# Pass back of a two-direction scan: centring and output product as plain fp32 quarter products

## The chip, the cores and the metric

The kernel runs on one core of one Trainium2 chip. The metric is device time in microseconds of that core for the whole computation. The kernel before took 10529.74 us (median of 3 runs, 10524.03 to 10529.78).

## What is computed

Input is an image batch x of shape (4, 64, 256, 256) in fp32. Layer 0 is a group norm and a convolution block, added to x. Layer 1 is a group norm and two state-space blocks, along rows and along columns, fused by a 1x1 product and added to x. The part that the change touches is the second half of the state-space block, for each direction:

```python
def _s5_block(x, i, ...):
    fx = _layer_norm(x, ln1_g[i], ln1_b[i])
    h = _s5_scan(fx, ...)                      # forward and backward scan, C product, D * u
    x = jax.nn.gelu(h) + fx
    fx2 = _layer_norm(x, ln2_g[i], ln2_b[i])   # centring, variance, scaling
    return fx2 @ ff_enc[i].T @ ff_dec[i].T + fx2
...
y = jnp.concatenate([y_h, y_v], axis=1)
return jnp.einsum('bihw,oi->bohw', y, fusion_w) + fusion_b[None, :, None, None]
```

Everything behind the second layer norm is linear, so the kernel folds it into one 64x64 matrix W per direction, with the centring in it; it is applied to the value before the norm, and the result is multiplied by one over the deviation afterwards.

## The kernel before

The sequence of one image has 65536 pixels of 64 channels. A tile is 128 partitions by 512 columns: the channels of one pixel parity on partitions 0 to 63, those of the other on 64 to 127. A pixel's channel vector thus lies on one half of the partitions, and a matrix that acts on channels is block diagonal over 128 partitions.

For each of 4 images the program does layer 0 (`l0_*`), then for direction 1 (columns) and 0 (rows) a pass ahead (`pa_*`: first layer norm, input product, forward scan) and a pass back (`pb_*`). A pass back has M = 64 steps, four (`s`) to each of 16 groups (`n`); there are 8 pass backs, 512 steps. The order on every engine is written out by hand, and engines meet through semaphores with counted values.

A step m of the pass back on TensorE (`pb_pe`), in the order of issue: `first(m)` (L1726, 12 fp32r products of 128x128 weights `Dwr` over 512 columns), `var(m-2)` (L1301, four fp32 products of 32 weight columns each over 128 columns, one to each quarter of the output partitions), `bc(m-6)` (L1308, four products that spread one over the deviation), `second(m)` (L1739, 6 products with `Cwr`), and `center(m-1)`: two products with `ctrr` into ps2 (L1748) and three with `WWr` into ps6 or ps7 (L1753). An fp32 value goes through the array as fp32r in two parts, a high and a low one, and a product with split weights takes three (`PARTS`).

What goes into `center`: ScalarE (`pb_act`) does the gelu from the bank of L1739 into `x2` (L1814), VectorE (`pb_dve`, `add`) adds the normed input (L1874), ScalarE copies it rounded into `xp[0]` (L1831), VectorE (`low`) subtracts it to make `xp[1]` (L1880). What comes out: ScalarE squares the centred value into `sr` (L1820) for `var`, and moves W's output into one of eight slots of `tW` (L1827). When four steps' variances are there, ScalarE takes the root, VectorE makes `RS` (`deviations`, L1295 to L1297), `bc` spreads it, VectorE multiplies (`norm`, L1886), six steps (`LAG`) behind `add`. GpSimd (`pb_pool`) adds the result to `av` (`fin_v`, direction 1) or `ah` (`fin_h`, direction 0); `interleave` adds the bias and orders the pixels for the store. VectorE further does the backward scan (L1851), its rotation (L1670 to L1673) and the parts of `XP` for the next group.

The weights come from the set-up: `CC` holds them in fp32, `split` writes the two parts to `CP`, and SP stores these as `kc_d` and loads them for each pass (`pa_sp`). `ps` are the eight PSUM banks of 128 partitions by 512 fp32. Two lines of `center` carry what is changed:

```python
for x in range(2):
    ins = e.matmul(ps[2][:], ctrr[:], xp[x][:], start=(x == 0), stop=(x == 1))
...
for w, x in PARTS:
    ins = e.matmul(ps[6 + m % 2][:], WWr[:, w, :], xp[x][:], start=(w == 0 and x == 0), stop=(w == 1))
```

Of the kernel before, what the change touches and what calls it, by code (L numbers as in the profile page):

```python
# [18 lines left out]
M = 4 * NG  # L19
# [91 lines left out]
def build(nc, a, NB):  # L111
# [23 lines left out]
    ctrr = at("ctrr", [128, 128], F32R)  # L135
    En, Bc = at("En", [128, 129]), at("Bc", [128, 2048], F32R)
    lows = En[:, 128:129]
# [106 lines left out]
    WWr = at("WWr", [128, 2, 128], F32R)  # L244
# [20 lines left out]
    x2 = at("x2", [128, 512])  # L265
    xp = [at(f"xp{p}", [128, 512], F32R) for p in range(2)]
# [28 lines left out]
    LOADS = 26  # L295
    STORES = 11

    def setup_sp(e):
        for dst, src in [
                (sel[:], a["k_sel"]), (pm1[:], a["k_pm1"]), (C2[:], a["C2"]),  # L300
                (ctr, a["k_ctr"]), (En[:], a["k_E"]), (Bc0[:], a["k_Bc"]), (idn[:], a["k_id"]),
                (par[:], a["par"]), (Bt[:], a["Bt"]), (BB[:], a["BB"]), (Ct[:], a["Ct"]), (Dv[:], a["Dv"]),
                (wdw[:], a["wdw"]), (wd, a["wd42"]), (winT[:], a["winT"]), (fwT[:], a["fwT"]), (woT[:], a["woT"][128:HID, :]),
                (woT0[:], a["woT"][0:128, :]), (enc[:], a["enc"]), (decT[:], a["decT"]), (wfT[:], a["wfT"]),
                (fb[:], a["fb"]), (g2[:], a["g2"]), (b2[:], a["b2"]), (g1[:], a["g1"]), (b1[:], a["b1"])]:
            e.dma_start(dst, src).then_inc(sem["ld"], 16)
# [5 lines left out]
        for i, c in enumerate((slice(0, 2048), slice(2048, 4224))):  # L312
            e.wait_ge(sem["parts"], i + 1)
            for dr in range(2):
                for p in range(2):
                    e.dma_start(kc_d[dr, p, :, c], CP[p][:, dr, c].bitcast(F32)).then_inc(sem["kst"], 16)
        e.wait_ge(sem["LW"], 1)
# [4 lines left out]
    def setup_dve(e, own):  # L322
# [221 lines left out]
        split(2048, 4224, 2)  # L544
        step(e.tensor_copy(ctrr[:], ctr))
# [715 lines left out]
    def pa_sp(e, b, d):  # L1261
# [8 lines left out]
        for g in range(NG + 1):  # L1270
# [4 lines left out]
            if g == NG:  # L1275
                e.wait_ge(sem["ctr"], M * (f + 1))
                for p in range(2):
                    e.dma_start(Dwr[:, p, :].bitcast(F32), kc_d[d, p, :, 2048:4096]).then_inc(sem["kD"], 16)
                    e.dma_start(WWr[:, p, :].bitcast(F32), kc_d[d, p, :, 4096:4224]).then_inc(sem["kD"], 16)
# [19 lines left out]
    def variances(e, o, i, src):  # L1299
        for q in range(4):  # L1300
            ins = e.matmul(o[32 * q:32 * q + 32, 0:128], En[:, 32 * i:32 * i + 32], src[:, 128 * q:128 * q + 128],  # L1301
                           start=(i == 0), stop=(i == 3))
        return ins
# [18 lines left out]
    def pa_pe(e, b, d):  # L1322
# [14 lines left out]
        def var(g, i):  # L1337
# [5 lines left out]
            variances(e, ps[2], i, sq[:, i % 2, :]).then_inc(sem["var"], 1)  # L1343
# [242 lines left out]
    def pb_sp(e, b, d):  # L1586
# [9 lines left out]
        def load_v(n):  # L1596
            if n >= 2:
                e.wait_ge(sem[f"avs{n % 2}"], 16 * (8 * b + (n - 2) // 2 + 1))
            e.dma_start(av[n % 2][:].rearrange("p v h w -> p (v h w)"),
                        x1v_d[b, order[n]].rearrange("p c v h w -> (p c) (v h w)")).then_inc(sem[f"av{n % 2}"], 16)  # L1600

        def load_h(n):
            g = order[n]
            for p in range(2):
                if n >= 2:
                    e.wait_ge(sem["il"], M * b + 4 * (n - 2) + 2 * p + 2)
                for v in range(2):
                    e.dma_start(ah[n % 2][64 * v:64 * v + 64, p, :].rearrange("c (k r) -> c k r", k=16),
                                acc_d[b, :, p, :, v, 8 * g:8 * g + 8, :].rearrange("k c h w -> c k (h w)")
# [65 lines left out]
    def fin_v(e, b, m):  # L1675
        n, s = divmod(m, 4)
        e.wait_ge(sem["n2"], M * phase(b, 1) + m + 1)
        if s == 0:
            e.wait_ge(sem[f"av{n % 2}"], 16 * (8 * b + n // 2 + 1))
# [15 lines left out]
    def interleave(e, b, n, i):  # L1695
# [5 lines left out]
        x = ah[n % 2][64 * v:64 * v + 64, p, :].rearrange("c (k h w) -> c h k w", k=16, h=8)  # L1701
        y = oh[64 * p:64 * p + 64].rearrange("c h (k w v) -> c v h k w", k=16, v=2)[:, v]
        e.activation(y, x, ACT.Identity, bias=bias[64 * v:64 * v + 64]).then_inc(sem["il"], 1)

    def pb_pe(e, b, d):
# [5 lines left out]
        def first(m):  # L1711
            n, s = divmod(m, 4)
            if m == 0:
                e.wait_ge(sem["kD"], 64 * (f + 1))
# [40 lines left out]

        def var(m):
# [4 lines left out]
            variances(e, ps[4], s, sr).then_inc(sem["va"], 1)  # L1761
# [25 lines left out]
    def pb_act(e, b, d):  # L1787
# [9 lines left out]
        for m in range(M + 2 if d else M + 9):  # L1797
# [42 lines left out]
    def pb_dve(e, own, b, d):  # L1840
# [25 lines left out]
        def add(m):  # L1866
# [7 lines left out]
            e.scalar_tensor_tensor(x2[:], fi[n % 2][:, s, :], g1[:, d:d + 1], x2[:], ALU.mult, ALU.add).then_inc(sem["x2"], 1)  # L1874
# [19 lines left out]
        for m in range(M + 8):  # L1894
# [9 lines left out]
            if m < M:  # L1904
                low(m)
# [154 lines left out]
```

## Time and profile before

| | |
|---|---|
| median of 3 runs | 10529.74 us (10524.03 to 10529.78) |
| the profiled execution, its span | 10530.0 us |
| TensorE busy | 94% |
| VectorE busy | 82% |
| ScalarE busy | 54% |
| GpSimd busy | 17% |
| mean granted TensorE clock | 0.978 |

The profile is one execution, recorded by the hardware. PE is TensorE's products, PEld its weight loads, DVE is VectorE, ACT ScalarE, POOL GpSimd, SP SyncE. L and a number is a line of the kernel. A group line gives: line, engine, operation, written tile <- read tiles, the products' weights (rows * columns), shapes, xcount | busy us, mean ns of one | idle time of that engine just before them, and who ended it. A timeline line gives start us, duration us, engine, line, operation and count, and in brackets the idle time before it where there was some. Products overlap in the records, since each is shown from its start until it has left the array: the distance of two starts tells what a product costs, not its duration. A plain fp32 product appears as two records, an fp32r one as one.

### The profile page before, as it was taken

How to read it: one execution, taken by the hardware profiler on the slowest of the kernel's cores; microseconds unless marked ns; L12 is line 12 of the kernel's file. 1: busy time of each engine (PE TensorE's matmuls, PEld its weight loads, DVE VectorE, ACT ScalarE, POOL GpSimd, SP SyncE). 2: the span in 40 equal slices, each digit the busy share in tenths (PEclk: the TensorE clock that was granted, in tenths of full speed). 3: DMA queues.
4: the chain of work that ended last, by engine and by line, in shares of the span. 5: the costliest groups of instructions: out<-in, count | busy, mean ns of one | idle time of the engine just before them, and what ended most of it. 6: DMA issues, size and time to landing. Idle time of an engine off the chain costs nothing.

```text
span 10530.0 us, 160761 instructions
## 1 busy us (share of the span) xinstructions
PE 9857.4 (94%) x59942; PEld 7478.5 (71%) x59942; DVE 8606.3 (82%) x12871; ACT 5728.6 (54%) x9047; POOL 1787.3 (17%) x1824
## 2 busy tenths in 40 slices
PE   1999999999999999998989999899999999989998
PEld 1777766767777776675777777577677777757666
DVE  7788878978788887888878888888886888788787
ACT  0555544656655554454765555455575555446557
POOL 0000003333300001233320000223341000033333
PEclk9999999999999999999999999999999999999999
DMA  4667655465676765446567676534566666553555
GB/s 115 143 140 144 139 146 186 166 225 145 153 148 140 143 139 176 163 172 213 153 148 144 140 143 137 204 146 195 173 171 129 128 128 128 122 209 158 216 152 150
DMA packets 1276979, 1650.34 MB, mean 157 GB/s; under 512 B 837532, under 2 KB 1070380, under 8 KB 1174444
## 3 DMA queue, kind: packets, MB, share of 16 engines
q1 hardware_dynamic: 1276204, 1640.07, 58.6%
q8 instruction: 479, 7.85, 0.3%
q14 instruction: 296, 2.42, 0.1%
HBM read 786.71 MB, written 515.00 MB: 124 GB/s over the span
## 4 chain that ended last, share of the span: by engine, by line
PE 82%; DVE 11%; issue 2%; ACT 2%; DMA 1%; SPq 1%; POOL 1%; ACTq 0%; DVEq 0%; POOLq 0%
PE ps L819 14%; PE ps L1726 12%; PE ps L1739 7%; PE ps L789 6%; PE ps L1308 5%; PE ps L849 4%; PE ps L780 4%; PE ps L833 4%; PE ps L1753 3%; PE ps L1335 3%; DVE S L1508 3%; PE ps L1301 3%; PE ps L873 2%; PE ps L860 2%; PE ps L795 2%
## 5 line engine op out<-in xcount | busy, mean ns | idle before, releaser
L1131 DVE SCALAR_TENSOR_TENSOR F<-U,LW,F 106x512 f32<-106x512 f32 x2048 | 1536.0, 750 | 54.4
L1726 PE MATMUL ps<-fp,Dwr 128*128 128x512 f32 x6144 | 1471.4, 389 | 0.0
L1726 PEld LDWEIGHTS ps<-fp,Dwr 128*128 128x128 f32 x6144 | 1153.2, 188 | 239.6
L1109 DVE TENSOR_TENSOR Z<-ps,LW 128x340 f32<-128x340 f32 x1024 | 523.2, 511 | 822.7 <-PE ps L789 821.7
L943 ACT ACTIVATE XF<-ps 128x340 f32<-128x340 f32 x1024 | 464.5, 454 | 1116.2 <-PE ps L780 1116.2
L819 PE MATMUL ps<-P,WP 128*128 128x512 f32 x3072 | 905.7, 417 | 32.0 <-DMA H<-P 32.0
L819 PE MATMUL ps<-H,WP 128*128 128x512 f32 x3072 | 918.3, 421 | 0.0
L1308 PEld LDWEIGHTS ps<-RS,Bc 128*128 128x128 f32 x4096 | 573.8, 196 | 471.8 <-DVE RS L1297 228.4
L1739 PE MATMUL ps<-XP,Cwr 128*128 128x512 f32 x3072 | 829.8, 407 | 68.4 <-DVE XP L1863 68.4
L1308 PE MATMUL ps<-RS,Bc 128*128 128x128 f32 x4096 | 766.7, 312 | 132.0 <-DVE RS L1297 132.0
L1374 PE MATMUL ps<-fp,Bwr 128*128 128x512 f32 x3072 | 836.9, 410 | 20.4 <-DVE fp L1477 20.4
L1049 POOL TENSOR_SCALAR xo<-xo 64x512 f32<-64x512 f32 x4 | 6.0, 1499 | 4907.5 <-DVE xo L1165 4907.5
L1814 ACT ACTIVATE x<-ps,cst 128x512 f32<-128x512 f32 x512 | 351.4, 686 | 895.3 <-PE ps L1739 868.1
L1692 POOL TENSOR_TENSOR ah<-tW,ah 128x256 f32<-128x256 f32 x512 | 617.0, 1231 | 1057.9 <-DVE xp L1880 1035.8
L789 PE MATMUL ps<-XF,Rfwd 128*128 128x340 f32 x2048 | 754.4, 450 | 9.4 <-ACT XF L943 9.4
L995 ACT ACTIVATE xb<-P 64x1024 fp32r<-64x1024 f32 x512 | 541.6, 1058 | 332.4 <-DVE P L1099 325.0
L819 PEld LDWEIGHTS ps<-H,WP 128*128 128x128 f32 x3072 | 578.5, 188 | 175.5
L1682 POOL TENSOR_TENSOR av<-tW,av 128x512 f32<-128x512 f32 x256 | 493.3, 1932 | 1177.1 <-DVE xp L1880 1165.2
L1739 PEld LDWEIGHTS ps<-XP,Cwr 128*128 128x128 f32 x3072 | 553.4, 193 | 167.8 <-issue 77.8
L1874 DVE SCALAR_TENSOR_TENSOR x<-fx,g,x 128x512 f32<-128x512 f32 x512 | 382.8, 748 | 350.8 <-ACT x L1814 350.5
L780 PEld LDWEIGHTS ps<-WP,xb 128*128 128x128 f32 x4096 | 593.6, 191 | 96.9 <-issue 31.7
L971 ACT ACTIVATE U<-ps 106x390 f32<-106x390 f32 x768 | 381.5, 497 | 516.2 <-PE ps L833 505.6
(295 smaller groups left out, 21105.0 us busy)
## 6 DMA issues: line engine op xcount, KB each, us to landing
H<-P SPq DMA_DIRECT2D x512, 585.0 KB, 7.2
raw<-x SPq DMA_DIRECT2D x240, 640.0 KB, 11.6
fx_d<-fx SPq DMA_DIRECT2D x112, 1024.0 KB, 3.9
fl_d<-fp SPq DMA_DIRECT2D x112, 1024.0 KB, 5.3
fp<-fl_d SPq DMA_DIRECT2D x112, 1024.0 KB, 6.2
fx<-fx_d SPq DMA_DIRECT2D x112, 1024.0 KB, 5.4
x1h_d<-xo SPq DMA_DIRECT2D x256, 256.0 KB, 9.0
x1v_d<-xo SPq DMA_DIRECT2D x512, 128.0 KB, 7.9
```

Of the source, the lines that this page charges most:

```text
L780: ins = e.matmul(ps[6][:, HID * j:HID * j + HID], xb[t % 2][:, k:k + 128], w(p, W_FR, HID), start=(p == 0), stop=(p == 1))
L789: e.matmul(ps[6][:, 0:2 * HID], Rfwd[:], XF[n % 2][:], start=True, stop=True).then_inc(sem["fs"], 1)
L819: e.matmul(ps[2 + i][:], w(pw_, W_CONV + 128 * j, 128), m, start=(j == 0 and pw_ == 0 and px == 0), stop=False)
L995: ins = e.activation(dst, src, ACT.Copy)
L1109: e.tensor_tensor(Z[t % 2][:, 2 * c:2 * c + 2, :].rearrange("p a b -> p (a b)"), ps[6][:, 0:2 * HID], Wt, ALU.mult).then_inc(sem["z"], 1)
L1131: ins = e.scalar_tensor_tensor(o, u, wd[0:106, i:i + 1], o, ALU.mult, ALU.add)
L1308: ins = e.matmul(o[:, 128 * q:128 * q + 128], Bc[:, c:c + 128], RS[:, m % 2, :], start=True, stop=True)
L1374: ins = e.matmul(o[:], Bwr[:, w, 128 * (2 * s + j):128 * (2 * s + j) + 128], fp[g % 2][x][:, s, :], start=(s == 0 and w == 0 and x == 0), ...
L1682: e.tensor_tensor(o, t, o, ALU.add).then_inc(sem["finv"], 1)
L1692: ins = e.tensor_tensor(o, t, o, ALU.add)
L1726: ins = e.matmul(bank(m)[:], Dwr[:, w, c:c + 128], fq[n % 2][x][:, s2, :], start=(s2 == 0 and w == 0 and x == 0), stop=False)
L1739: ins = e.matmul(bank(m)[:], Cwr[:, w, c:c + 128], XP[x][:, j, :], start=False, stop=(j == 1 and w == 1))
```

## The change

Centring and W become plain fp32 products of 64x64, one for each half of the partitions. Centring takes rows 0 to 63 to output partitions 0 to 63 and rows 64 to 127 to 64 to 127; W takes rows 0 to 63 to output partitions 64 to 127 and the other way round, so the four products lie in four different quarters of the array. The value is kept in fp32 in two buffers `X2`, the high and low parts `xp` go, and with them L1831 and L1880. Since W swaps the two pixels of a tile, `variances` gets its own selection matrix `Es` in the pass back, and the loads of `av` and `ah` and the `interleave` swap the halves too. W's weights are stored and loaded whole instead of in parts.

```diff
-    ctrr = at("ctrr", [128, 128], F32R)
+    ctq = at("ctq", [128, 128])
+    Es = at("Es", [128, 128])
-    WWr = at("WWr", [128, 2, 128], F32R)
+    Wq = at("Wq", [128, 128])
-    x2 = at("x2", [128, 512])
-    xp = [at(f"xp{p}", [128, 512], F32R) for p in range(2)]
+    X2 = [at(f"x2{i}", [128, 512]) for i in range(2)]
-    LOADS = 26
-    STORES = 11
+    LOADS = 28
+    STORES = 13
@@ setup_sp
+        for dr in range(2):
+            e.dma_start(kc_d[dr, 0, :, 4096:4224], CC[:, dr, 4096:4224]).then_inc(sem["kst"], 16)
@@ setup_dve
-        split(2048, 4224, 2)
-        step(e.tensor_copy(ctrr[:], ctr))
+        split(2048, 4096, 2)
+        step(e.tensor_copy(ctq[:], ctr))
@@ pa_sp
-                    e.dma_start(WWr[:, p, :].bitcast(F32), kc_d[d, p, :, 4096:4224]).then_inc(sem["kD"], 16)
+                e.dma_start(Wq[:], kc_d[d, 0, :, 4096:4224]).then_inc(sem["kD"], 16)
@@ pb_sp, load_v
-            e.dma_start(av[n % 2][:].rearrange("p v h w -> p (v h w)"),
-                        x1v_d[b, order[n]].rearrange("p c v h w -> (p c) (v h w)")).then_inc(sem[f"av{n % 2}"], 16)
+            for p, hf in ((0, slice(64, 128)), (1, slice(0, 64))):
+                e.dma_start(av[n % 2][hf].rearrange("c v h w -> c (v h w)"),
+                            x1v_d[b, order[n], p].rearrange("c v h w -> c (v h w)")).then_inc(sem[f"av{n % 2}"], 16)
@@ pb_pe, center
-            e.wait_ge(sem["xp"], M * f + m + 1)
+            e.wait_ge(sem["x2"], M * f + m + 1)
             if m:
                 e.wait_ge(sem["sr"], M * f + m)
-            for x in range(2):
-                ins = e.matmul(ps[2][:], ctrr[:], xp[x][:], start=(x == 0), stop=(x == 1))
-            ins.then_inc(sem["cc"], 1)
             if m >= 2:
                 e.wait_ge(sem["tw"], M * f + m - 1)
-            for w, x in PARTS:
-                ins = e.matmul(ps[6 + m % 2][:], WWr[:, w, :], xp[x][:], start=(w == 0 and x == 0), stop=(w == 1))
+            for hf in (slice(0, 64), slice(64, 128)):
+                ins = e.matmul(ps[2][hf, :], ctq[hf, hf], X2[m % 2][hf, :], start=True, stop=True)
+            ins.then_inc(sem["cc"], 1)
+            for hf, other in ((slice(0, 64), slice(64, 128)), (slice(64, 128), slice(0, 64))):
+                ins = e.matmul(ps[6 + m % 2][other, :], Wq[hf, hf], X2[m % 2][hf, :], start=True, stop=True)
             ins.then_inc(sem["w"], 1)
@@ pb_act
-                if m:
-                    e.wait_ge(sem["xp"], M * f + m)
-                e.activation(x2[:], ps[{2: 3, 3: 5}.get(m, m % 2)][:], ACT.Gelu_apprx_tanh, bias=cD[:, 4 * d + s:4 * d + s + 1]
+                if m >= 2:
+                    e.wait_ge(sem["w"], M * f + m - 1)
+                e.activation(X2[m % 2][:], ps[{2: 3, 3: 5}.get(m, m % 2)][:], ACT.Gelu_apprx_tanh, bias=cD[:, 4 * d + s:4 * d + s + 1]
-            if m < M:
-                e.wait_ge(sem["x2"], M * f + m + 1)
-                e.activation(xp[0][:], x2[:], ACT.Copy).then_inc(sem["xp0"], 1)
@@ pb_dve
-        def low(m):
-            e.wait_ge(sem["xp0"], M * f + m + 1)
-            if m:
-                e.wait_ge(sem["w"], M * f + m)
-            e.tensor_tensor(xp[1][:], x2[:], xp[0][:].bitcast(F32), ALU.subtract).then_inc(sem["xp"], 1)
@@ pb_pool
-            e.wait_ge(sem["xp"], M * phase(b, d) + min(m + LAG + 1, M))
```

## Rows read from the trace of the kernel before

**Rows 1.** The page: busy time by engine, and the clock in 40 slices.
```profile
PE 9857.4 (94%) x59942; PEld 7478.5 (71%) x59942; DVE 8606.3 (82%) x12871; ACT 5728.6 (54%) x9047; POOL 1787.3 (17%) x1824
...
PEclk9999999999999999999999999999999999999999
```

**Rows 2.** Busy time in two pass-back stretches (stretch, length, busy us per engine, clock, DMA).
```profile
1779.00:2166.00 387.00, 383.53 (x2150) 296.81 (x2151) 335.32 (x471) 228.87 (x368) 111.41 (x58) 1.00 0.39 153
2433.00:2820.00 387.00, 383.07 (x2152) 296.19 (x2152) 323.35 (x471) 294.54 (x423) 146.05 (x129) 1.00 0.55 150
```

**Rows 3.** Timeline of TensorE over two steps of a pass back.
```profile
1806.03 1.58 PE L1739 MATMUL ps<-XP,Cwr 128*128 128x512 f32 x6
1807.45 0.61 PE L1748 MATMUL ps<-xp,ctrr 128*128 128x512 f32 x2
1807.90 0.84 PE L1753 MATMUL ps<-xp,WWr 128*128 128x512 f32 x3
1808.59 2.88 PE L1726 MATMUL ps<-fp,Dwr 128*128 128x512 f32 x12
1811.40 0.43 PE L1301 MATMUL ps<-sr,En 128*32 128x128 f32 x8
1811.75 0.66 PE L1308 MATMUL ps<-RS,Bc 128*128 128x128 f32 x4
1812.25 1.58 PE L1739 MATMUL ps<-XP,Cwr 128*128 128x512 f32 x6
1813.67 0.61 PE L1748 MATMUL ps<-xp,ctrr 128*128 128x512 f32 x2
...
1819.89 0.61 PE L1748 MATMUL ps<-xp,ctrr 128*128 128x512 f32 x2
```

**Rows 4.** Timeline around L873 and, narrow windows, in L873 and L1301.
```profile
1006.44 0.57 PE L780 MATMUL ps<-WP,xb 128*128 128x170 f32 x4
1006.74 0.28 PE L780 MATMUL ps<-WP,xb 128*128 128x170 f32 x1
1006.95 1.08 PE L873 MATMUL ps<-F,LW 128*64 128x512 f32 x4
1006.95 0.65 PE L873 MATMUL ps<-F,LW 128*64 128x512 f32 x2
1007.43 0.60 PE L873 MATMUL ps<-F,LW 128*64 128x512 f32 x2
1007.96 0.96 PE L876 MATMUL ps<-FQ,WO 106*128 106x512 f32 x3
1008.75 0.73 PE L789 MATMUL ps<-XF,Rfwd 128*128 128x340 f32 x2
...
2004.22 0.32 PE L1301 MATMUL ps<-sr,En 128*32 128x128 f32 x4
2004.35 0.29 PE L1301 MATMUL ps<-sr,En 128*32 128x128 f32 x4
```

**Rows 5.** Groups of products by line, and two lines' durations min/median/max.
```profile
L1748 PE MATMUL ps<-xp,ctrr 128*128 128x512 f32 x1024 | 319.1, 393 | 31.2 <-DVE xp L1880 31.2
L1335 PE MATMUL ps<-xin,Mb 128*128 128x512 f32 x1024 | 552.5, 643 | 12.2 <-DMA xin<-x1v_d 12.1 <-ACT xc L1422 0.2
...
L1748 PE MATMUL ps<-xp,ctrr x1024: 387/389/627, 1779.5 to 10493.6; 128*128 128x512 f32 x171
L1335 PE MATMUL ps<-xin,Mb x1024: 590/592/1222, 1517.7 to 10054.5; 128*128 128x512 f32 x171
```

**Rows 6.** Timeline where TensorE waits in a pass back, and the scans.
```profile
1779.48 0.74 PE L1748 MATMUL ps<-xp,ctrr 128*128 128x512 f32 x2 [0.64 <-DVE xp L1880]
1784.92 0.96 PE L1748 MATMUL ps<-xp,ctrr 128*128 128x512 f32 x2 [1.89 <-DVE xp L1880]
1997.37 3.92 DVE L1851 TENSOR_TENSOR_SCAN S<-RR,S 64x512 f32<-64x512 f32 x2
2165.33 0.73 PE L1748 MATMUL ps<-xp,ctrr 128*128 128x512 f32 x2 [0.80 <-DVE xp L1880]
2170.85 3.80 PE L1308 MATMUL ps<-RS,Bc 128*128 128x128 f32 x16 [2.98 <-DVE RS L1297]
2433.35 0.73 PE L1748 MATMUL ps<-xp,ctrr 128*128 128x512 f32 x2 [1.51 <-DVE xp L1880]
2438.79 0.73 PE L1748 MATMUL ps<-xp,ctrr 128*128 128x512 f32 x2 [1.92 <-DVE xp L1880]
2442.78 0.74 PE L1748 MATMUL ps<-xp,ctrr 128*128 128x512 f32 x2 [0.45 <-DVE xp L1880]
```

**Rows 7.** Groups of the copy and the subtraction.
```profile
L1831 ACT ACTIVATE xp<-x 128x512 fp32r<-128x512 f32 x512 | 325.2, 635 | 285.9 <-DVE x L1874 285.5
L1880 DVE TENSOR_TENSOR xp<-x,xp 128x512 fp32r<-128x512 f32 x512 | 353.0, 689 | 96.4 <-ACT xp L1831 76.2
```

More of the change, by code:

```diff
@@ L300, in setup_sp @@
                 (sel[:], a["k_sel"]), (pm1[:], a["k_pm1"]), (C2[:], a["C2"]),
-                (ctr, a["k_ctr"]), (En[:], a["k_E"]), (Bc0[:], a["k_Bc"]), (idn[:], a["k_id"]),
+                (ctr, a["k_ctr"]), (En[:], a["k_E"]), (Es[0:64], a["k_E"][64:128, 0:128]), (Es[64:128], a["k_E"][0:64, 0:128]), (Bc0[:], a["k_Bc"]), (idn[:], a["k_id"]),
                 (par[:], a["par"]), (Bt[:], a["Bt"]), (BB[:], a["BB"]), (Ct[:], a["Ct"]), (Dv[:], a["Dv"]),
@@ L311, in setup_sp @@
             e.dma_start(tb_d[dr], TB[:, dr].rearrange("p a b -> p (a b)")).then_inc(sem["kst"], 16)
-        for i, c in enumerate((slice(0, 2048), slice(2048, 4224))):
+        for i, c in enumerate((slice(0, 2048), slice(2048, 4096))):
             e.wait_ge(sem["parts"], i + 1)
@@ L1297, in deviations, with variances @@
         e.scalar_tensor_tensor(RS[:, m % 2, :], rh[:].bitcast(F32), lows, rs[:], ALU.mult, ALU.add).then_inc(sem[out], 1)
-    def variances(e, o, i, src):
+    def variances(e, o, i, src, pick):
         for q in range(4):
-            ins = e.matmul(o[32 * q:32 * q + 32, 0:128], En[:, 32 * i:32 * i + 32], src[:, 128 * q:128 * q + 128],
+            ins = e.matmul(o[32 * q:32 * q + 32, 0:128], pick[:, 32 * i:32 * i + 32], src[:, 128 * q:128 * q + 128],
                            start=(i == 0), stop=(i == 3))
@@ L1342, in var @@
                 e.wait_ge(sem["sd"], NG * f + g)
-            variances(e, ps[2], i, sq[:, i % 2, :]).then_inc(sem["var"], 1)
+            variances(e, ps[2], i, sq[:, i % 2, :], En).then_inc(sem["var"], 1)
         def bc(g, i):
@@ L1606, in load_h @@
                     e.wait_ge(sem["il"], M * b + 4 * (n - 2) + 2 * p + 2)
-                for v in range(2):
-                    e.dma_start(ah[n % 2][64 * v:64 * v + 64, p, :].rearrange("c (k r) -> c k r", k=16),
-                                acc_d[b, :, p, :, v, 8 * g:8 * g + 8, :].rearrange("k c h w -> c k (h w)")
+                for v, hf in ((0, slice(64, 128)), (1, slice(0, 64))):
+                    e.dma_start(ah[n % 2][hf, p, :].rearrange("c (k r) -> c k r", k=16),
+                                acc_d[b, :, 1 - p, :, v, 8 * g:8 * g + 8, :].rearrange("k c h w -> c k (h w)")
                                 ).then_inc(sem[f"ah{n % 2}"], 16)
@@ L1678, in fin_v @@
         if s == 0:
-            e.wait_ge(sem[f"av{n % 2}"], 16 * (8 * b + n // 2 + 1))
+            e.wait_ge(sem[f"av{n % 2}"], 32 * (8 * b + n // 2 + 1))
         o = av[n % 2][:].rearrange("p v (j s) w -> p s v w j", s=4)[:, s]
@@ L1700, in interleave @@
                 e.wait_ge(sem["ost"], 32 * (NG * b + n))
-        x = ah[n % 2][64 * v:64 * v + 64, p, :].rearrange("c (k h w) -> c h k w", k=16, h=8)
+        hf = slice(64, 128) if v == 0 else slice(0, 64)
+        x = ah[n % 2][hf, p, :].rearrange("c (k h w) -> c h k w", k=16, h=8)
         y = oh[64 * p:64 * p + 64].rearrange("c h (k w v) -> c v h k w", k=16, v=2)[:, v]
-        e.activation(y, x, ACT.Identity, bias=bias[64 * v:64 * v + 64]).then_inc(sem["il"], 1)
+        e.activation(y, x, ACT.Identity, bias=bias[hf]).then_inc(sem["il"], 1)
     def pb_pe(e, b, d):
@@ L1713, in first @@
             if m == 0:
-                e.wait_ge(sem["kD"], 64 * (f + 1))
+                e.wait_ge(sem["kD"], 48 * (f + 1))
                 e.wait_ge(sem["sq"], M * (f + 1))
@@ L1760, in var @@
                 e.wait_ge(sem["se"], NG * f + n)
-            variances(e, ps[4], s, sr).then_inc(sem["va"], 1)
+            variances(e, ps[4], s, sr, Es).then_inc(sem["va"], 1)
         def bc(m):
@@ L1873, in add @@
                     e.wait_ge(sem["nn"], M * (f + 1))
-            e.scalar_tensor_tensor(x2[:], fi[n % 2][:, s, :], g1[:, d:d + 1], x2[:], ALU.mult, ALU.add).then_inc(sem["x2"], 1)
-        def low(m):
-            e.wait_ge(sem["xp0"], M * f + m + 1)
-            if m:
-                e.wait_ge(sem["w"], M * f + m)
-            e.tensor_tensor(xp[1][:], x2[:], xp[0][:].bitcast(F32), ALU.subtract).then_inc(sem["xp"], 1)
+            e.scalar_tensor_tensor(X2[m % 2][:], fi[n % 2][:, s, :], g1[:, d:d + 1], X2[m % 2][:], ALU.mult, ALU.add
+                                   ).then_inc(sem["x2"], 1)
         def norm(m):
@@ L1903, in pb_dve @@
                 norm(m - LAG)
-            if m < M:
-                low(m)
             if s == 0 and n + 1 < NG:
```

2 rows, old and new, of the table SEMAPHORES are left out of this document.

## The prediction

> **What bounds the kernel now.** I read the page first: busy shares, then the clock line [rows 1]. TensorE is busy 94% of the span, VectorE 82%, ScalarE 54%, and the clock stands at its upper level (2.4 GHz) nearly throughout. Shares do not say what one stage waits for, so I took two pass-back stretches by themselves [rows 2]: in 387.0 us TensorE is busy 383 us, VectorE 335 and 323, ScalarE 229 and 295. Each stretch is one of eight pass backs (4 images, 2 directions) of 64 steps; all the change's work lies in these 512 steps. The timeline of TensorE in two neighbouring steps [rows 3] shows a fixed pattern with no wait printed: 12 products of L1726, the variances L1301, the spreading L1308, 6 products of L1739, then centring L1748 and W L1753. From 1807.45 to 1813.67 is 6.22 us, and so is the next. In steady state the step is the sum of TensorE's own work: what is added there is paid in full, what is taken from ScalarE or VectorE is not earned. Waits of TensorE stand only at the ends of a pass back [rows 6].
>
> **What TensorE gives up.** Per step 2 + 3 fp32r products of 128x128 weights over 512 columns. By the timeline they hold TensorE from 1807.45 to 1808.59 = 1.14 us, 0.227 each [rows 3]. Nothing lies beside them.
>
> **What it gets instead.** Four plain fp32 products with 64 rows and 64 columns: two on the diagonal quarters (centring, bank ps2), two on the other quarters (W, bank ps6 or ps7). No row of before has a product on a quarter; this is the disputed term, so it is bounded.
> - Alone: fp32 records come in two per product, and L1335 costs 552.5 us for 512 products, 1.08 us each [rows 5]. Four one after another, each at 1.08: 4.3 us.
> - Side by side: L873 is two fp32 products of 64 columns over 512, in the two column halves. In the narrow looks [rows 4] two records of different halves are under way together from 1006.95, and the other two from 1007.43. So the column halves work at the same time, in two waves 0.48 us apart. L1301 does the same with four tiles of 32 columns: four records at 2004.22, four at 2004.35 [rows 4]. The four quarters are also four tiles; if they behave like these four, they too need two waves.
> - The price of such a visit is more than its waves. Around L873 [rows 4]: the four L780 start at 1006.44 to 1006.74, 0.10 apart, but L873 starts 0.21 after the last, so 0.11 is lost going in; L873 holds the engine 1.01 (1006.95 to 1007.96); then three L876 take 0.79 to the next start against 3 x 0.227 = 0.68, so 0.11 is lost coming out. Sum 1.23 us. L1301 behind L1726 agrees in kind: 12 products from 1808.59 should be over at 1811.31, and it starts at 1811.40 [rows 3].
>
> I take the two waves and 1.22 us (each of the three differences is good to 0.01), since L873 and L1301 are the nearest rows (same type, same 512 columns, tiles below full width). A quarter has half the rows of L873, so a slightly shorter drain is possible, and two more weight loads per wave, so a slightly longer entry; I let these cancel. Step: 1.22 - 1.14 = +0.08 us. Over 512 steps: **+41 us**. The bounds around it: the waves alone, without entry and exit, are 2 x 0.43 = 0.86 (the 0.43: an fp32 record lasts 592 ns against 389 for an fp32r one [rows 5], 0.203 longer than one that is spaced 0.227), which is 0.28 less than now; with the full 0.37 of L873 and 0.15 more for four weight loads it is 1.38, 0.24 more.
>
> Beside this, "TensorEngine Tiling (Array Packing)" of the Trainium skill, Key Properties, says that changing the tiling mode drains TensorE, and that tiles then work independently. The trace agrees: the 0.11 us on either side of L873 are such changes, and they speak against this change, which adds two per step. Without them the term would be a gain.
>
> **What leaves the other engines.** ScalarE loses the copy L1831 (512 x 635 ns), VectorE the subtraction L1880 (512 x 689 ns) [rows 7]. In steady steps both lie beside TensorE's work: worth 0. The value is double-buffered, so gelu L1814 waits for W of two steps earlier instead of the subtraction; worth 0 too. With them the path gelu, add, centring is 0.64 + 0.69 = 1.32 us shorter, which counts where TensorE really waits for it. That is 31.2 us in all, before L1748 [rows 5]: at the start of a pass back 0.64 + 1.89, or 1.51 + 1.92 + 0.45, and 0.80 at its end [rows 6]. At the start the two small steps fall away before the pair of scans of 3.9 us [rows 6] that VectorE does between the first two values, so the second value gains twice and these waits should go: 31.2 - 8 x 0.80 = 24.8 us. At the end the wait of 0.80 goes, but centring itself tells ScalarE later (two fp32r took 0.61 to their end, two waves take 1.08 as in L873 [rows 4]), 0.47 later; the chain to the last deviations (L1308 waits 2.98 us for RS [rows 6]) keeps only some 0.3, 8 times, 2.6 us. Together **-27 us**. Late next at the start: TensorE itself.
>
> **What is moved or small.** Centring now also waits for tw of two steps earlier ahead of itself; behind it on TensorE stand W and the next L1726, but tw is long done (ScalarE is busy 3.7 us of 6.2 per step). GpSimd's last addition follows n2 instead of xp, in the same VectorE turn; it is 1.9 us long in a 6.2 us step. SP's queue: one load of 64 KB less per pass back, and each 1 MB load of av goes in two halves; it is issued a group of four steps (25 us) ahead. The set-up gets two small loads and two small stores: +1 us at most, before the first meeting. The swapped pixels change addresses only.
>
> **Sum.** Against the profiled execution: 10530.0 + 41 - 27 + 0 = 10544; its span stands 0.3 us above the median of the runs, 10529.74, so **10543 us**. That is +0.13%; about 0.2%, 21 us, is what a measurement of this kernel can tell from no change.
>
> **The rivals.**
> 1. *Only pairs are concurrent*: the two quarters of centring work together, and then those of W, because the row halves get in each other's way. Then four waves: 2 x 0.43 us more per step, +440 us: 10984. For it: no row shows row halves at work together. Against it: L1301 runs four tiles. A rule of the skill leads there: its tiling page, Gotcha 1, says that different row tiles cannot use one PSUM bank at the same time, and here both row halves write ps2 and ps6; whether a different partition half is enough no run here shows.
> 2. *Three waves*: W's first records start with centring's second ones, since a semaphore stands between the pairs. One wave more, 512 x 0.43 = 220 us: 10763. Against it: nothing waits between the pairs.
> 3. *All four in series*: eight waves, 6 x 0.43 = 2.6 us more: about 11865. L873 speaks against it for columns, nothing for rows.
> 4. *The visit is cheaper* than L873's: half the rows, half the drain. With the entry and exit at half (0.18 instead of 0.37) the step is 1.03 to 1.04, 0.10 to 0.11 less than now: -56 - 27 = -83, 10447.
> 5. *The other engines were the bound* and their relief is the gain: 0.69 us of VectorE in each of 512 steps would be 353 us, 10177. The waits of TensorE (3.3 to 4.7 us of 387 [rows 2, 6]) exclude it, so it gets no chance.
>
> **How the numbers follow.** The forecast mechanism (two waves, about L873's price) 0.72; rival 4 0.11; rival 1 0.07; rival 2 0.07; rival 3 0.03. Within the forecast the price of a visit is uncertain by some 0.06 us per step, 30 us in all: its own range is 10485 to 10605, and over the bounds of 21 us this splits 0.13 faster, 0.34 within, 0.25 slower. So faster 0.24, same 0.34, slower 0.42 (0.25 and 0.17). The range goes from 10460 (half of rival 4) to 10780 (rival 2), which leaves out rivals 1 and 3 and the rest of 4, under 2 in 10.
>
> **What would show it.** In the changed kernel's narrow looks, centring's and W's first records (two and two) start within some 0.05 us of each other, the second ones 0.43 to 0.48 later: two waves. The distance from centring's start to the next L1726 start is 1.01 (plus 0.11 in front and behind), where it is 1.14 now, and the steady step is 6.30. If the step is 6.7, rival 2; 7.2, rival 1; 8.9, rival 3; 6.1, rival 4. The waits before centring at the start of a pass back are gone, and VectorE's share falls by some 3 points. The forecast is wrong if a steady step shows a wait of TensorE, or if the row halves do not work together.

## The result, and the profile after

| | kernel before | changed kernel |
|---|---|---|
| median of five runs (lowest to highest) | 10529.46 us (10519.9 to 10529.78) | 10562.84 us (10561.22 to 10564.83) |
| span of the profiled execution | 10530.0 us | 10563.0 us |
| ratio to before, 95% interval | | 1.0034 [1.0023, 1.0044] |

The changed kernel is 33 us slower (+0.3%, beyond the 0.2% that can be told from no change). The forecast was 10543 us, 20 us less; the range of 10460 to 10780 holds the time.

The page of the changed kernel, the lines that answer [rows 1]:

```profile
PE 9902.3 (94%) x61478; PEld 7065.4 (67%) x61478; DVE 8286.4 (78%) x12359; ACT 5480.0 (52%) x8535; POOL 1756.9 (17%) x1824
...
PEclk6999999999999999999999999999999999999999
```

VectorE lost 320 us of work and ScalarE 249 us, and the kernel did not become faster: TensorE has as large a share as before. The 6 in the first slice of the clock lies in the set-up, ahead of every pass back, and costs nothing: the first pass back begins at 1751.29 us (L1730), where it began at 1754.83 (L1726).

The same two pass-back stretches (columns as in [rows 2]):

```profile
1776.00:2166.00 390.00, 387.50 (x2333) 244.34 (x2332) 293.89 (x407) 198.71 (x305) 110.19 (x57) 1.00 0.46 149
2433.00:2824.00 391.00, 388.67 (x2342) 245.09 (x2344) 282.85 (x407) 262.51 (x359) 141.55 (x128) 1.00 0.54 149
```

TensorE idles 2.5 and 2.3 us of some 390, where it idled 3.5 and 3.9 of 387: what waits there were went, and the work itself grew. The timeline of TensorE in the changed kernel shows where, against [rows 3]:

```profile
1807.02 1.58 PE L1743 MATMUL ps<-XP,Cwr 128*128 128x512 f32 x6
1808.53 0.65 PE L1754 MATMUL ps<-x,ctq 64*64 64x512 f32 x2
1808.55 0.65 PE L1757 MATMUL ps<-x,Wq 64*64 64x512 f32 x2
1809.01 0.59 PE L1754 MATMUL ps<-x,ctq 64*64 64x512 f32 x2
1809.03 0.60 PE L1757 MATMUL ps<-x,Wq 64*64 64x512 f32 x2
1809.55 3.03 PE L1730 MATMUL ps<-fp,Dwr 128*128 128x512 f32 x12
1812.51 0.43 PE L1303 MATMUL ps<-sr,Es 128*32 128x128 f32 x8
1812.87 0.66 PE L1310 MATMUL ps<-RS,Bc 128*128 128x128 f32 x4
1813.37 1.58 PE L1743 MATMUL ps<-XP,Cwr 128*128 128x512 f32 x6
1814.88 0.65 PE L1754 MATMUL ps<-x,ctq 64*64 64x512 f32 x2
...
1821.23 0.65 PE L1754 MATMUL ps<-x,ctq 64*64 64x512 f32 x2
```

L1754 (centring) and L1757 (W) start their first records within 0.02 us of each other and their second ones 0.48 later: four quarters, two waves. From centring to the next L1730 is 1.02 us, and two steps from 1808.53 to 1821.23 take 12.70, so a step is 6.35 us where it was 6.22. Of the 0.13, L1730 has its part: its group of 12 lasts 3.03 where L1726's lasted 2.88. Two windows that begin behind the first two of the twelve leave the start of the group aside; first the kernel before, then the changed one:

```profile
1809.04 2.43 PE L1726 MATMUL ps<-fp,Dwr 128*128 128x512 f32 x10
```
```profile
1810.12 2.47 PE L1730 MATMUL ps<-fp,Dwr 128*128 128x512 f32 x10
```

One fp32r record lasts 0.39 us and the others follow at even starts, so the spacing is (2.43 - 0.39) / 9 = 0.227 us before and (2.47 - 0.39) / 9 = 0.231 after. The operands of these products and their shapes did not change. The first of the eleven distances is 0.335, the way out of the quarters. Of the ten behind it eight are longer than 0.227 (0.228 to 0.236) and one is shorter (0.225), in the same places of every step, 0.041 us together.

The groups of the changed kernel by line (busy, mean ns of one | idle before them and its releaser), against [rows 5]:

```profile
L1730 PE MATMUL ps<-fp,Dwr 128*128 128x512 f32 x6144 | 1542.6, 400 | 0.0
L1754 PE MATMUL ps<-x,ctq 64*64 64x512 f32 x2048 | 551.5, 615 | 0.6 <-DVE x L1875 0.5
L1303 PE MATMUL ps<-sr,Es 128*32 128x128 f32 x4096 | 218.1, 285 | 28.3 <-ACT sr L1824 28.3
```

The same for the kernel before:

```profile
L1726 PE MATMUL ps<-fp,Dwr 128*128 128x512 f32 x6144 | 1471.4, 389 | 0.0
L1301 PE MATMUL ps<-sr,En 128*32 128x128 f32 x4096 | 219.0, 286 | 7.4 <-ACT sr L1820 6.0
```

The 31.2 us that TensorE waited before centring are 0.6 now. In their place the variances wait 28.3 us for the square of the centred value instead of 7.4.

### The profile page after: what moved, and what is told of

It reads as the page before. It is cut to its first block, busy times and chain, and to the rows that moved or that the text cites. A ratio compares the mean times of both kernels' runs of the same rounds, so it can differ in the third digit from the quotient of the medians.

```text
span 10563.0 us, 161973 instructions
## 1 busy us (share of the span) xinstructions
PE 9902.3 (94%) x61478; PEld 7065.4 (67%) x61478; DVE 8286.4 (78%) x12359; ACT 5480.0 (52%) x8535; POOL 1756.9 (17%) x1824
## 4 chain that ended last, share of the span: by engine, by line
PE 83%; DVE 11%; issue 2%; ACT 1%; DMA 1%; SPq 1%; POOL 1%; ACTq 0%; DVEq 0%; POOLq 0%
PE ps L821 14%; PE ps L1730 13%; PE ps L1743 7%; PE ps L791 6%; PE ps L1754 5%; PE ps L1310 5%; PE ps L851 4%; PE ps L782 4%; PE ps L835 4%; PE ps L1337 3%; DVE S L1510 3%; PE ps L1303 3%; PE ps L875 2%; PE ps L862 2%; PE ps L797 2%
## 5 line engine op out<-in xcount | busy, mean ns | idle before, releaser
L1730 PE MATMUL ps<-fp,Dwr 128*128 128x512 f32 x6144 | 1542.6, 400 | 0.0
L1730 PEld LDWEIGHTS ps<-fp,Dwr 128*128 128x128 f32 x6144 | 1115.5, 188 | 612.6 <-ACT x L1818 249.9
L1743 PE MATMUL ps<-XP,Cwr 128*128 128x512 f32 x3072 | 827.7, 406 | 70.2 <-DVE XP L1864 70.2
L1310 PE MATMUL ps<-RS,Bc 128*128 128x128 f32 x4096 | 767.4, 312 | 130.6 <-DVE RS L1299 130.6
L1310 PEld LDWEIGHTS ps<-RS,Bc 128*128 128x128 f32 x4096 | 574.4, 197 | 470.2 <-issue 233.0
L1743 PEld LDWEIGHTS ps<-XP,Cwr 128*128 128x128 f32 x3072 | 551.7, 193 | 168.2 <-issue 79.6
```

The source lines that it names most:

```text
L1310: ins = e.matmul(o[:, 128 * q:128 * q + 128], Bc[:, c:c + 128], RS[:, m % 2, :], start=True, stop=True)
L1730: ins = e.matmul(bank(m)[:], Dwr[:, w, c:c + 128], fq[n % 2][x][:, s2, :], start=(s2 == 0 and w == 0 and x == 0), stop=False)
L1743: ins = e.matmul(bank(m)[:], Cwr[:, w, c:c + 128], XP[x][:, j, :], start=False, stop=(j == 1 and w == 1))
```

## Experiments

Theory: a step is the sum of TensorE's own work; a visit to the quarters is two concurrent waves plus a fixed price for going in and out; the relief of ScalarE and VectorE pays only at the ends of a pass back. The rivals that were still alive: the two waves have another ground than the four quarters; the slower spacing of L1730 comes from the tiling, or from the other engines; the order of the step could win back what the visit costs. Measured beside the experiments, the kernel before took 10529.83 us (13 runs, beside the first four kernels) and 10528.13 us (9 runs, beside the last four).

### One quarter's place: W on the same quarters as centring

```diff
-  ins = e.matmul(ps[6 + m % 2][other, :], Wq[hf, hf], X2[m % 2][hf, :], start=True, stop=True)
+  ins = e.matmul(ps[6 + m % 2][hf, :], Wq[hf, hf], X2[m % 2][hf, :], start=True, stop=True)
```

> The changed kernel with W in the same two quarters as centring (W's output goes to the partitions it came from, so the two pixels of each tile are exchanged in the result). Theory: in the changed kernel all four quarters work at the same time, in two waves 0.48 us apart. Here W has to follow centring in its quarters: four waves, 2 x 0.43 us more, step 7.2 us instead of 6.35, about 11000 us. Rival: a product of 64 rows and 64 columns is simply short, and the quarters do nothing for each other: then the order of quarters does not matter, and the time stays at 10563.

Measured 10961.75 us (one run). The timeline of TensorE in this kernel:

```profile
1852.57 1.08 PE L1754 MATMUL ps<-x,ctq 64*64 64x512 f32 x4
1853.48 1.02 PE L1757 MATMUL ps<-x,Wq 64*64 64x512 f32 x4
1854.44 3.01 PE L1730 MATMUL ps<-fp,Dwr 128*128 128x512 f32 x12
...
1859.74 0.65 PE L1754 MATMUL ps<-x,ctq 64*64 64x512 f32 x2
```

Centring's four records take two waves, and W's come 0.91 later: four waves. From centring to the next L1730 it is 1.87 us instead of 1.02, and L1730, with fewer long distances here, gives some 0.02 back: the step is 7.17 us, 0.82 above that of the changed kernel. The concurrency of all four is real, and it is worth some 400 us: it is what keeps the change near the time before.

### No quarters: the same products plain fp32 over the whole array

```diff
-  for hf in (slice(0, 64), slice(64, 128)):
-      ins = e.matmul(ps[2][hf, :], ctq[hf, hf], X2[m % 2][hf, :], start=True, stop=True)
+  e.matmul(ps[2][:], ctq[:], X2[m % 2][:], start=True, stop=True).then_inc(sem["cc"], 1)
...
-  for hf, other in ((slice(0, 64), slice(64, 128)), (slice(64, 128), slice(0, 64))):
-      ins = e.matmul(ps[6 + m % 2][other, :], Wq[hf, hf], X2[m % 2][hf, :], start=True, stop=True)
+  ins = e.matmul(ps[6 + m % 2][:], Wq[:], X2[m % 2][:], start=True, stop=True)
```

> The changed kernel with centring and W as plain fp32 products of the whole 128x128 block-diagonal matrices (W's pixels not exchanged, so the result has the pixels of each tile swapped). There is no change of tiling around them and nothing side by side. Theory: four records one after another, 4 x 0.43 = 1.72 us, with no entry and exit, where the changed kernel needs 1.22: step 6.35 + 0.50 - 0.04 = 6.81, about 10800 us, and the 12 products of L1730 behind them are spaced 0.227 us again (they are 0.224 to 0.236 in the changed kernel). Compared with the four waves of the run in the same quarters, the difference is the price of the changes of tiling, 0.35 us per step. Rival for the slower L1730: the other engines' new timing disturbs it. Then it stays at 0.231 here, and the time is 10820.

Measured 10809.05 us (one run). TensorE's timeline, and a window with the last eleven of a group of L1730:

```profile
1852.72 1.02 PE L1753 MATMUL ps<-x,ctq 128*128 128x512 f32 x2
1853.57 1.02 PE L1754 MATMUL ps<-x,Wq 128*128 128x512 f32 x2
...
1859.57 1.02 PE L1753 MATMUL ps<-x,ctq 128*128 128x512 f32 x2
```
```profile
1861.52 2.70 PE L1730 MATMUL ps<-fp,Dwr 128*128 128x512 f32 x11
```

The step is 6.85 us and the time between the two that were expected (10800 and 10820). Four fp32 records one after another on the whole array cost 0.32 us less than four waves of quarters (7.17). The price of a visit by itself is some 0.03 more, 0.35, since the long distances of this kernel add that much over those of the quarters' kernel. But the spacing stays at (2.70 - 0.39) / 10 = 0.231 us, where 0.227 was expected. So the slower L1730 is not the tiling's.

### The relief alone: no copy, no subtraction, old products

```diff
-                ins = e.matmul(ps[2][:], ctrr[:], xp[x][:], start=(x == 0), stop=(x == 1))
+                ins = e.matmul(ps[2][:], ctrr[:], xp[m % 2][:], start=(x == 0), stop=(x == 1))
...
-                ins = e.matmul(ps[6 + m % 2][:], WWr[:, w, :], xp[x][:], start=(w == 0 and x == 0), stop=(w == 1))
+                ins = e.matmul(ps[6 + m % 2][:], WWr[:, w, :], xp[m % 2][:], start=(w == 0 and x == 0), stop=(w == 1))
...
-                e.activation(xp[0][:], x2[:], ACT.Copy).then_inc(sem["xp0"], 1)
...
-            e.scalar_tensor_tensor(x2[:], fi[n % 2][:, s, :], g1[:, d:d + 1], x2[:], ALU.mult, ALU.add).then_inc(sem["x2"], 1)
+            e.scalar_tensor_tensor(xp[m % 2][:], fi[n % 2][:, s, :], g1[:, d:d + 1], x2[:], ALU.mult, ALU.add).then_inc(sem["x2"], 1)
...
-            e.tensor_tensor(xp[1][:], x2[:], xp[0][:].bitcast(F32), ALU.subtract).then_inc(sem["xp"], 1)
```

> The kernel before without ScalarE's rounding copy and VectorE's subtraction: the addition writes the rounded value itself, in two buffers, and the five fp32r products read it twice (the low part of the value is left out). TensorE's instructions are those of before. Theory: in a steady step the relief is worth nothing (6.22 us); at the ends of the eight pass backs TensorE's waits before centring go, 31.2 us in all, of them 27 to 31 earned: about 10500. Rival (the other engines bound the step): the step itself becomes shorter, up to 0.69 us, 10180.

Measured 10489.43 us (four runs), ratio 0.9963 [0.995, 0.9977]. The low part of the value is left out of its products, all five of which run. The relief is worth 39 us, and the rest of the change costs 10562.84 - 10489.43 = 73. Group of centring, and a window with eleven of L1726:

```profile
L1748 PE MATMUL ps<-xp,ctrr 128*128 128x512 f32 x1024 | 317.8, 392 | 1.4 <-DVE xp L1873 1.4
```
```profile
1854.79 2.65 PE L1726 MATMUL ps<-fp,Dwr 128*128 128x512 f32 x11
```

The waits are gone, and the spacing is (2.65 - 0.39) / 10 = 0.226 us. This kernel and the full-array one have the same work on ScalarE and VectorE and neither has quarters; they differ in fp32 against fp32r products ahead of the twelve, and with that the spacing changes. Since the relief alone leaves it at 0.226, it is not the relief of the other engines that slows L1730.

The 39 us are more than the waits of 31.2 us. A part of the rest is in the first steps. The kernel before, five microseconds round its second wait (columns as in [rows 2]) and what TensorE did there:

```profile
1784.00:1789.00 5.00, 4.08 (x17) 2.59 (x18) 3.82 (x6) 2.73 (x5) 0.00 (x0) 0.66 0.00 0
```
```profile
1785.67 1.48 PE L1753 MATMUL ps<-xp,WWr 128*128 128x512 f32 x3
1787.67 2.10 PE L1739 MATMUL ps<-XP,Cwr 128*128 128x512 f32 x6
```

The relief alone at the same place of the pass back:

```profile
1778.00:1783.00 5.00, 5.00 (x29) 4.05 (x22) 4.96 (x10) 2.27 (x4) 0.00 (x0) 1.00 0.11 13
```
```profile
1778.14 1.66 PE L1739 MATMUL ps<-XP,Cwr 128*128 128x512 f32 x6
1780.09 0.84 PE L1753 MATMUL ps<-xp,WWr 128*128 128x512 f32 x3
```

After its waits of 0.64 and 1.89 us [rows 6] TensorE in the kernel before had 0.66 of its clock, part of those five microseconds at 1.2 and not 2.4 GHz, and L1753 took 1.48 us instead of 0.84. Without the waits the clock stays at 1.00. But the slow stretch does not follow every such wait: in the kernel before it shows in four of the eight pass backs, and the pass back at 2433, with longer waits (1.51, 1.92 and 0.45 us [rows 6]), has none:

```profile
2438.00:2443.00 5.00, 3.66 (x20) 2.29 (x21) 4.22 (x7) 2.89 (x6) 0.00 (x0) 1.00 0.01 2
```

By stretches of the two profiled executions, all eight pass backs together: from the first L1726 to that of the ninth step the relief saves 29.5 us, of which 22 are idle time of TensorE, so the clock is worth 7 at most. From there to the last step it saves nothing (6.22 us a step in both), and behind that 6.0.

### The relief undone: copy and subtraction put back into the changed kernel

```diff
+  e.activation(dm[:], X2[m % 2][:], ACT.Copy).then_inc(sem["xp0"], 1)
+  e.tensor_tensor(dm[:], X2[m % 2][:], dm[:], ALU.subtract).then_inc(sem["xp"], 1)
...
-  e.wait_ge(sem["x2"], M * f + m + 1)
+  e.wait_ge(sem["xp"], M * f + m + 1)
```

The last two lines are the wait ahead of centring.

> The changed kernel with the copy on ScalarE and the subtraction on VectorE put back, into a spare buffer, and centring waiting for the subtraction; TensorE's products are those of the change. Theory: the steady step stays at 6.35, the waits at the ends come back: 10563 + 22 to 30 = 10585 to 10593. L1730's spacing tells of its cause: if it is TensorE's own affair, it stays at 0.231; if it came from the other engines' changed timing, it goes back to 0.227 and the step to 6.31, and the time to about 10570.

Measured 10612.22 us (four runs), ratio 1.008 [1.0066, 1.0094]: 49 us above the changed kernel, at least 19 more than expected. The group of centring:

```profile
L1755 PE MATMUL ps<-x,ctq 64*64 64x512 f32 x2048 | 551.6, 615 | 39.0 <-DVE dm L1886 38.3
```

38 of the 49 us are waits (39.0 for 0.6). They are not at the ends alone: in the four pass backs of direction 1 about every fourth step is 6.62 to 6.67 us instead of 6.35, some 15 us in all. There the deviations stand ahead of the addition and the subtraction on VectorE. And the relief is not undone as it was; the subtraction takes far longer than the 689 ns of L1880 [rows 7]:

```profile
L1886 DVE TENSOR_TENSOR dm<-x,dm 128x512 f32<-128x512 f32 x512 | 646.6, 1263 | 161.0 <-ACT dm L1838 140.8
```

It lasts 0.69 us in the first steps, where GpSimd rests, and behind them, in three steps of four of that pass back, 1.5 to 2.2, with GpSimd's addition L1686 under way beside it (at 1850.99 us it lasts 2.22). As in the changed kernel, that addition follows L1892 and no longer the subtraction, so that the two now meet. That they slow each other is argued from this; no run separates them. So this run puts an upper bound on what the relief is worth, and the 39 us of the run before are its measure. The spacing of L1731 is 0.231 as without the copy, so the copy and the subtraction do not change it.

### Another order: centring ahead of the variances

```diff
+  if 1 <= m <= M:
+      center(m - 1)
...
-  if 1 <= m <= M:
-      center(m - 1)
```

> The changed kernel with the quarter products moved from behind L1743 to directly in front of the variances L1303, so that two tiled visits stand next to each other and TensorE goes to full width once per step less. Theory (the changes of tiling are what eats the gain): one exit (0.10 us and 0.11 us for an exposed weight load) and one entry (0.10) fall away, some 0.1 is left for the change between the two tilings: 0.2 us x 480 = 96 us less, about 10465 us, a step of 6.15. Rival: the change from quarters to 32-column tiles costs as much as the two it replaces, 10563. Rival: centring now has only the 2.8 us of L1730 between gelu's input and itself; gelu 0.69 and add 0.75 fit, but where VectorE scans or ScalarE loads a table they do not; then waits of TensorE before centring appear in one step of four and the time is 10500 to 10560.

Measured 10527.68 us (ten runs), ratio to before 0.9998 [0.9989, 1.0008]. The step is 6.16 us: the quarters and the 32-column tiles of L1303 stand next to each other and share a way in and out. But the rival by which TensorE waits was right; the group of centring, a wait in the first steps of a pass back, and then the timeline of VectorE and TensorE at a wait further on:

```profile
L1754 PE MATMUL ps<-x,ctq 64*64 64x512 f32 x2048 | 557.0, 621 | 61.4 <-DVE x L1875 55.1
```
```profile
1780.80 0.65 PE L1754 MATMUL ps<-x,ctq 64*64 64x512 f32 x2 [1.64 <-DVE x L1875]
```
```profile
1899.63 0.95 DVE L1297 RECIPROCAL rs<-rs 128x128 f32<-128x128 f32 x1
...
1900.88 0.35 DVE L1299 SCALAR_TENSOR_TENSOR RS<-rh,En,rs 128x128 fp32r<-128x128 f32 x1
...
1901.15 0.75 DVE L1875 SCALAR_TENSOR_TENSOR x<-fx,g,x 128x512 f32<-128x512 f32 x1
...
1901.95 0.65 PE L1754 MATMUL ps<-x,ctq 64*64 64x512 f32 x2
```

Centring now comes earlier in the step than the value does. Most of the waiting stands in the first steps, where no L1730 lies between gelu and centring: 38 of the 61.4 us are waits there, 11 lie in the steps between and 12 at the ends. In the steps between, every fourth one of direction 1, the deviations stand ahead of the addition on VectorE from 1899.63, and TensorE stands still until the addition is through.

### That order from the fifth step on, and the addition ahead of the deviations

```diff
+  if 4 <= m <= M:
+      center(m - 1)
...
-  if 1 <= m <= M:
+  if 1 <= m < 4:
       center(m - 1)
...
-  if s == 1 and 1 <= n <= NG:
-      deviations(e, own, n - 1, "se", NG * f + n, "rsb")
...
+  if s == 1 and 1 <= n <= NG:
+      deviations(e, own, n - 1, "se", NG * f + n, "rsb")
```

> The changed kernel with the quarter products directly ahead of the variances as in the run before, but only from step 4 on (the first steps keep the old order, where no L1730 lies between gelu and centring), and with VectorE's addition ahead of the deviations in each fourth step. Theory: the step is 6.16 everywhere, TensorE's 55 us of waits before centring go but for some 10: 10528 - 45 = 10483. Rival: the deviations, now 0.75 us later, make the spreading wait, or the scan does what the deviations did, and 10510 to 10528 is left.

Measured 10476.63 us (five runs), ratio to before 0.9952 [0.9938, 0.9966]. It is faster than both kernels: 52 us below before, 86 below the change. TensorE's timeline and the group of centring:

```profile
1852.33 0.65 PE L1754 MATMUL ps<-x,ctq 64*64 64x512 f32 x2
...
1853.34 0.43 PE L1303 MATMUL ps<-sr,Es 128*32 128x128 f32 x8
...
1858.48 0.65 PE L1754 MATMUL ps<-x,ctq 64*64 64x512 f32 x2
```
```profile
L1754 PE MATMUL ps<-x,ctq 64*64 64x512 f32 x2048 | 551.2, 615 | 13.5 <-DVE x L1877 13.2
```

The step from 1852.33 to 1858.48 is 6.15 us, and the waits fell from 61.4 to 13.5: 48 of the 51 us by which this kernel is faster than the other order alone. Both causes found in that run are confirmed by their cures, the first one as the larger: the old order in the first steps takes 37 us of waits away, the addition ahead of the deviations the 11 of the steps between. What is left lies at the ends.

### Two looks at the slower L1730

The spreading L1310 moved behind centring, so that it stands between the quarters and L1730:

```diff
-  if m >= LAG:
-      bc(m - LAG)
...
+  if m >= LAG:
+      bc(m - LAG)
```

> The changed kernel with the four spreading products L1310 moved behind the quarter products, so that L1730 no longer follows a tiled visit directly. The exposed weight loads only change places (0.054 us before L1310, 0.108 before L1743 or L1730). Theory A: L1730's slower spacing (0.231 instead of 0.227, 0.04 us per step) is what a stream of full-width products pays right behind a tiled visit; the spreading takes it, L1730 is spaced 0.227, and the time is 10563 - 20 = 10543. Theory B: it is contention with the other engines during L1730; it stays, 10563.

Measured 10574.36 us (four runs), ratio 1.0044 [1.0029, 1.0059]; neither number. The step, from centring to centring:

```profile
1853.06 0.65 PE L1754 MATMUL ps<-x,ctq 64*64 64x512 f32 x2
...
1854.08 0.67 PE L1310 MATMUL ps<-RS,Bc 128*128 128x128 f32 x4
1854.58 2.98 PE L1730 MATMUL ps<-fp,Dwr 128*128 128x512 f32 x12
...
1859.44 0.65 PE L1754 MATMUL ps<-x,ctq 64*64 64x512 f32 x2
```

6.38 us against 6.35. The long distances are still there behind four other products, and there are some in L1743 too, which now follows the variances directly (0.228 to 0.236, where all were 0.227). So it is not the place right behind the quarters that is slow, and the variances, plain fp32 products too, have long distances behind them as well.

Each quarter product cut into two of 256 columns:

```diff
+  for h in (slice(0, 256), slice(256, 512)):
-      ins = e.matmul(ps[2][hf, :], ctq[hf, hf], X2[m % 2][hf, :], start=True, stop=True)
+      ins = e.matmul(ps[2][hf, h], ctq[hf, hf], X2[m % 2][hf, h], start=True, stop=True)
```

W's are cut likewise.

> The changed kernel with each of the four quarter products cut into two of 256 columns: twice the instructions (32 instead of 16), the same columns through the array. Question: why are the nine L1730 behind the visit slower (0.229 to 0.236 for 0.227)? Theory A (instructions: TensorE's sequencer has to catch up after a burst): more than nine of the twelve are slow, the step grows by 0.02 to 0.05 us on that account, with 0.03 for the two more waves' starts: 10580 to 10600. Theory B (the fp32 streaming itself, by what it draws): the number stays at nine, and the time at 10565 to 10580.

Measured 10561.22 us (one run), the changed kernel's time, and neither expectation: only four of the ten distances behind the first are long in most steps, where eight should have stayed or more have come, and the cut into 256 columns costs 0.02 us (centring to L1730, 1.04 for 1.02), which the spacing gives back. How many distances are long also varies elsewhere without a rule that I can name: eight in the change, the full-array kernel and the undone relief; four where W shares centring's quarters and in the first steps of a pass back, which have no spreading. With centring ahead of the variances four are long in L1743 and five in L1730, and from the third distance of L1743 on they are, in order and within 0.001 us, those that the changed kernel has in L1730 alone (0.229, 0.234, 0.235, 0.225, 0.230, 0.236, 0.229, 0.232, 0.231). So it is one fixed sequence that runs on through the next full-width products of 512 columns; where only four are long in L1730, with W on centring's quarters and with half columns, they are its last four.

The kernel before has such distances as well, in the pass ahead, where L1374 follows plain fp32 products; four of its products:

```profile
1606.57 1.09 PE L1374 MATMUL ps<-fp,Bwr 128*128 128x512 f32 x4
```

They are (1.09 - 0.39) / 3 = 0.233 us apart, where L1726 has 0.227. The change did not bring the slower spacing about; it moved it into the pass back.

## Why the prediction was right or wrong

**What bounds the kernel: right.** VectorE fell by 4 points and ScalarE by 2 for no gain in a steady step, and the step grew by what TensorE got. The rival by which the relief is worth 353 us is excluded: alone it was 39.

**The visit to the quarters: right, in kind and size.** The rows of L873 carried over: two waves 0.48 us apart, 1.02 us from centring to the next product. Going in costs 0.09: from the six L1743 to centring it is 1.51 us (1807.02 to 1808.53), where from the six L1739 it was 1.42 [rows 3]. Coming out costs 0.11: the twelve L1730 last 2.96 to the start of L1303 (1809.55 to 1812.51), where they lasted 2.81, and 0.04 of the 0.15 is their spacing. So a visit is 0.09 + 1.02 + 0.11 = 1.22 us, as forecast, against 1.13 to 1.14 that went: +0.086 x 512 = 44 us, forecast 41. Rivals 1 to 3 fall with the narrow starts (0.02 apart, not 0.5), and their prices stand: the kernel that forces four waves has a step of 7.17 where rival 1 said 7.2. Rival 4 falls with the 1.02. Two figures beside the sum were off. The 4.3 us for four products in series took 1.08 us, the time of a lone product with its tail, for a spacing; in the full-array kernel the next product starts after 0.85 (1852.72 to 1853.57). And the 0.15 us for four weight loads in the upper bound is shown by no run: going in costs 0.09 in all.

In rival 1 I had weighed a rule of the Trainium skill, page "TensorEngine Tiling (Array Packing)", Gotcha 1, by which different row tiles cannot use one PSUM bank at the same time. This case's trace does not agree: the two row halves wrote ps2 and ps6 side by side, in different partition halves, with starts 0.01 to 0.02 us apart. Its Key Properties, that a change of tiling mode drains TensorE, agree with the trace: some 0.35 us per visit by the two experiments above, and 0.19 us of the step won where two tiled groups stand together.

**The products behind it: the step that failed.** My sum had every other product of TensorE at its old spacing. The twelve fp32r products take 0.041 us more per step, some 20 us in all, and that is the distance from 10543 to 10563. The kernel before had it on record: L1374 is spaced 0.233 behind plain fp32 products, and the 0.79 us of the three L876 behind L873 [rows 4], which I read as the way out alone, hold a little of it. The sum priced the visit and not the products behind it. The full-array kernel (slow) against the relief alone (clean) ties it to plain fp32 products of 512 columns earlier in the step; the relief alone, the undone relief and the moved spreading exclude the copy and the subtraction on the other engines and the place next to the quarters. What inside TensorE does it stays open, and so does the count of long distances.

**The relief at the ends: right sign, 12 us too small.** The run says 39 us, not 27. By stretches the starts of the pass backs gave 29.5 where I had 24.8, and the ends 6.0 where I had 2.6. At the starts I had taken the waits at their own length, and the clock that fell to 0.66 behind some of them cost up to 7 us more. The remaining 4 us lie outside the pass backs, most of them in the set-up (L616 starts at 207.1 us instead of 210.8), and no trace ties them to the relief. The clock line of the page [rows 1] shows nothing of the slow stretches, since a slice is 263 us long; it took windows of 5 us.

**Centring reports later: right place, too small.** I had 0.47 us at the end of a pass back only, and let the chain hide part of it. It also falls at the start, where nothing is queued between. Rows of the changed kernel at the start and at the end of one pass back:

```profile
1778.03 0.43 PE L1303 MATMUL ps<-sr,Es 128*32 128x128 f32 x8 [0.78 <-ACT sr L1824]
...
1782.08 0.43 PE L1303 MATMUL ps<-sr,Es 128*32 128x128 f32 x8 [0.77 <-ACT sr L1824]
```
```profile
2165.81 0.43 PE L1303 MATMUL ps<-sr,Es 128*32 128x128 f32 x8 [0.77 <-ACT sr L1824]
...
2168.62 0.42 PE L1303 MATMUL ps<-sr,Es 128*32 128x128 f32 x8 [0.78 <-ACT sr L1824]
```

Four waits of 0.78 in each of eight pass backs are 25 of the group's 28.3 us; with the relief alone that group waited 10.6. So up to 18 us; by the balance, +33 = 44 + 20 - 39 + 8, some 8 of them lengthen the kernel. The stretches agree: starts and ends of the eight pass backs are together 16 us longer in the changed kernel than with the relief alone, and the longer step explains 9 of them (72 steps of 0.127), which leaves 7.

**Taken together.** The forecast of +14 missed 3 us at the visit, 20 at the spacing, -12 at the relief and 8 at the late centring: 19 in sum. The last two nearly cancel; the spacing alone is as large as the bound between no change and slower, and so it decided the verdict. The order of the work on TensorE and VectorE, which the change left as it was, is worth more than any of these terms: 86 us.

## What to carry to other kernels

Read the step as one engine's sum before counting what the others lose, and price a tiled visit as waves plus the way in and out (some 0.35 us in this kernel), and read the spacing of the products behind it too; put tiled groups side by side, so that the price falls once. If a product is moved earlier in its engine's order, look at what makes its operand, and move that too. Where an engine waits more than a microsecond at a stage's start, look at its clock in windows of a few microseconds: the wait can cost more than its length.

## What was not expected of the hardware

- Two row halves of the array write different partition halves of the same PSUM bank at the same time (starts 0.02 us apart, all four quarters in two waves, 2 x 0.48 us). The rows of before showed this for column halves only.
- fp32r products of 128x128 over 512 columns start every 0.227 us, but some 0.231 on average behind plain fp32 products of 512 columns (2.70 us against 2.65 for eleven), on quarters and on the whole array. The distances follow a fixed sequence over up to ten products. The cause is open.
- Plain fp32 products on tiles can be cut from 512 to 2 x 256 columns for 0.02 us per visit.
- The granted clock fell to 0.66 in a window of 5 us behind two short waits (0.64 and 1.89 us) in a stage that is otherwise 99% busy; it did so in four of eight pass backs, and not in one with longer waits.
- VectorE's subtraction of 128x512 values took 0.69 us with GpSimd at rest and up to 2.22 us with GpSimd's addition beside it (the undone relief; that the addition is the cause is argued, not shown).
